# Turning the mixed graph weights K on TensorE in float32 instead of by a DMA transpose

## The reference, cut to what matters

```
x = layernorm(x + first_layer(x, adj))                # h in the kernel, per item [128, 512]
z_l, z_g, v = h @ W_lang.T, h @ W_grav.T, h @ W_V.T
A_l = relu(cos(z_l, z_l)) * not_eye ;  A_g = exp(-|z_g - z_g|^2 / (2 sigma^2)) * not_eye
K_l, K_g = A * adj mask / row sum, for each
K   = w_l * K_l + (1 - w_l) * K_g                     # [128, 128] per item
out = layernorm(h + (K @ v) @ W_O.T)
```

## Time and profile before

| | |
|---|---|
| median of 3 runs | 918.71 us |
| the profiled execution | 919.98 us, its span 918.2 us |
| busy: TensorE, VectorE, ScalarE, GpSimd | 97%, 79%, 63%, 35% |
| granted TensorE clock, mean | 0.994 |
| DMA | 79.55 MB in all; 74 DMA transposes |

### The profile page before, as it was taken

The page is one execution under the profiler, slowest core; times in us unless marked ns, Lnnn a source line. Parts: engine busy times, 40 slices in busy tenths (PEclk is TensorE's granted clock), DMA queues, the critical chain, the costliest instruction groups (busy, mean ns, idle before and its releaser), DMA issues.

```text
span 918.2 us, 18540 instructions
## 1 busy us (share of the span) xinstructions
PE 894.0 (97%) x6706; PEld 535.7 (58%) x6706; DVE 726.8 (79%) x1681; ACT 580.3 (63%) x1069; POOL 321.4 (35%) x306
## 2 busy tenths in 40 slices
PE   8999999999999999999999999999999999999995
PEld 6777886565555555556565656555555555655452
DVE  5888488868788778788788878888878787878867
ACT  6987676697565566665656575757575747472623
POOL 4888353045232333232424242424242424240300
PEclk9999999999999999999999999999999999999998
DMA  8554220201423232323233323233323323241311
GB/s 302 206 183 131 100 93 13 77 5 28 88 70 93 70 91 69 91 71 89 77 92 74 98 68 104 61 101 63 107 57 103 65 95 70 91 65 51 58 46 47
DMA packets 105113, 79.55 MB, mean 87 GB/s; under 512 B 81904, under 2 KB 82032, under 8 KB 103152
## 3 DMA queue, kind: packets, MB, share of 16 engines
q1 hardware_dynamic: 105072, 79.02, 31.5%
HBM read 42.80 MB, written 16.81 MB: 65 GB/s over the span
## 4 chain that ended last, share of the span: by engine, by line
PE 53%; DVE 14%; DMA 6%; ACT 4%; issue 4%; POOL 3%; SPq 1%; DVEq 0%; ACTq 0%; POOLq 0%
PE bank L261 11%; PE bank L263 11%; PE bank L262 11%; PE pair L261 6%; PE pair L263 6%; PE pair L262 6%; DMA arena<-in_x 3%; POOL arena L442 2%; DMA arena<-arena 1%; SPq L333 1%; DVE arena L1783 1%; DMA arena<-rn_dram 1%; DVE stats L1726 1%; DVE arena L1773 1%; DMA rn_dram<-nl 1%
## 5 line engine op out<-in xcount | busy, mean ns | idle before, releaser
L261 PE MATMUL bank<-arena 128*128 128x512 f16 (+2 forms) x1056 | 290.5, 300 | 5.3 <-DMA arena<-arena 4.2
L262 PE MATMUL bank<-arena 128*128 128x512 f16 (+2 forms) x1056 | 291.2, 300 | 0.0
L263 PE MATMUL bank<-arena 128*128 128x512 f16 (+2 forms) x1056 | 291.2, 300 | 0.0
L438 POOL TENSOR_TENSOR arena<-arena 128x512 f32<-128x512 f32 x60 | 76.3, 1271 | 229.5 <-ACT arena L1090 229.5
L261 PE MATMUL pair<-arena 128*128 128x512 f16 (+1 forms) x400 | 150.4, 376 | 0.0
L262 PE MATMUL pair<-arena 128*128 128x512 f16 (+1 forms) x400 | 150.4, 376 | 0.0
L263 PE MATMUL pair<-arena 128*128 128x512 f16 (+1 forms) x400 | 150.3, 376 | 0.0
L261 PEld LDWEIGHTS bank<-arena 128*128 128x128 f16 x1056 | 103.3, 98 | 66.9 <-DMA arena<-arena 5.6
L263 PEld LDWEIGHTS bank<-arena 128*128 128x128 f16 x1056 | 103.3, 98 | 62.9
L262 PEld LDWEIGHTS bank<-arena 128*128 128x128 f16 x1056 | 103.3, 98 | 58.5 <-issue 0.7
L452 POOL TENSOR_TENSOR arena<-arena 128x512 f16<-128x512 f32 x56 | 64.9, 1160 | 170.1 <-ACT arena L1075 170.1
(11 more groups left out here) (368 smaller groups left out, 1880.2 us busy)
## 6 DMA issues: line engine op xcount, KB each, us to landing
arena<-in_x SPq DMA_DIRECT2D x32, 1024.0 KB, 5.6
out_dram<-arena SPq DMA_DIRECT2D x15, 1024.0 KB, 4.3
arena<-rn_dram SPq DMA_DIRECT2D x15, 256.0 KB, 3.8
arena<-arena SPq DMA_TRANSPOSE x74, 3.2
arena<-in_x SPq DMA_DIRECT2D x2, 512.0 KB, 4.6
arena<-in_w_grav_t SPq DMA_DIRECT2D x1, 1024.0 KB, 7.4
arena<-in_w_lang_t SPq DMA_DIRECT2D x1, 1024.0 KB, 5.5
arena<-in_w_v SPq DMA_DIRECT2D x1, 1024.0 KB, 8.4
```

The costliest lines, as they stand in the source:

```text
L261: pe.matmul(dst, ah, bh, start=start, stop=False)
L262: pe.matmul(dst, ah, bl, start=False, stop=False)
L263: return pe.matmul(dst, al, bh, start=False, stop=stop)
L438: pool.tensor_tensor(y[:, b, :], y[:, b, :], xg[slot][:, b, :], ALU.add).then_inc(s["y_ready"], 1)
```

## The change

All groups now turn K the way of group 14: TensorE's `turn_k(g)` stands behind the first quarter of the last value product, VectorE makes both float16 parts out of bank 6. ScalarE's high part of K, VectorE's low part out of SBUF, the tile `k_parts`, the DMA transpose and the semaphore `kT_in` are gone. `project_ahead` writes bank 6 (its item 2), so it waits there for `kT_l_ready`. `k_gravity` (ScalarE) no longer waits for the DMA transpose of the group before.

```diff
@@ SyncE: turn_k removed
-            def turn_k(g):
-                sp.wait_ge(s["kT_l_ready"], g + 1)
-                wait(sp, s["out_ps"], g * GB)
-                sp.dma_start_transpose(kT, k_parts.rearrange("p b n -> p (b n)")).then_inc(s["kT_in"], 16)
             def turn_h(g, slot):
...
-                    if b == HALF and g < NG - 1:
-                        turn_k(g - 1)
@@ TensorE
             def project_ahead(g):
...
                 for b in range(GB):
+                    if b == HALF:
+                        wait(pe, s["kT_l_ready"], g - 1)
                     project_x(g, b, x_h, x_l, bank[4 + b])
...
                 values(g, slot, 2)
+                values(g, slot, 3, range(0, 1))
+                turn_k(g)
+                values(g, slot, 3, range(1, KB))
                 if has_second:
-                    values(g, slot, 3)
                     project_ahead(g + 2)
-                    pe.wait_ge(s["kT_in"], g * 16 + 16)
-                else:
-                    values(g, slot, 3, range(0, 1))
-                    turn_k(g)
-                    values(g, slot, 3, range(1, KB))
-                    pe.wait_ge(s["kT_l_ready"], g + 1)
+                pe.wait_ge(s["kT_l_ready"], g + 1)
                 for b in range(GB):
                     weighted(g, b)
@@ ScalarE
                 act.wait_ge(s["cf_ready"], g + 1)
-                wait(act, s["kT_in"], turned)
...
                     first_norm(g + 1, 1 - slot, 2)
-                    act.wait_ge(s["k_ready"], g + 1)
-                    act.activation(k_parts[:, 0:GB, :], k_mix, ACT.Copy, scale=K_UP).then_inc(s["kT_h_ready"], 1)
                     first_norm(g + 1, 1 - slot, 3)
@@ VectorE
                 v_low(g, 0)
-                if has_second:
-                    dve.wait_ge(s["kT_h_ready"], g + 1)
-                    dve.scalar_tensor_tensor(k_parts[:, GB:, :], k_mix, K_UP, k_parts[:, 0:GB, :], ALU.mult,
-                                             ALU.subtract).then_inc(s["kT_l_ready"], 1)
-                else:
-                    dve.wait_ge(s["kT_ps"], 1)
-                    ...
+                dve.wait_ge(s["kT_ps"], g + 1)
+                dve.tensor_scalar(kT_h, bank[6][:].rearrange("p (b n) -> p b n", b=GB), K_UP, None,
+                                  ALU.mult).then_inc(s["kT_h_ready"], 1)
+                turned_k_low(g)
+                if not has_second:
                     dve.wait_ge(s["hh_ready"], g * GB + GB)
```

More of the change, by code:

```diff
@@ L233, in build @@
             at(next(tile_at), [GB, P]) for _ in range(10))
-        k_parts = at(100 * KIB, [2 * GB, P], F16)
         kT = at(108 * KIB, [2 * GB, P], F16)
@@ L252, in build @@
             dev_ready rn_spread rm_ps sq_ps rn_out rn_in hk_ready e_ready graph_steps cf_steps cf_ready k_ready kg_ready cl_ready
-            v_ps v_h_ready v_l_ready kT_ps kT_h_ready kT_l_ready kT_in o_first out_ps y2_ready
+            v_ps v_h_ready v_l_ready kT_ps kT_h_ready kT_l_ready  o_first out_ps y2_ready
             ln2_var ln2_log ln2_exp ln2_steps o_ready stored stats2_ready nl_steps2 stat1_steps stat2_steps""".split()
@@ L1222, in v_high, with k_gravity @@
                 act.activation(v_h[:, b, :], bank[b][:], ACT.Copy, scale=V_DOWN).then_inc(s["v_h_ready"], 1)
-            def k_gravity(g, turned):
+            def k_gravity(g):
                 act.wait_ge(s["cf_ready"], g + 1)
-                wait(act, s["kT_in"], turned)
                 for b in range(GB):
@@ L1273, in body @@
                 first_roots(g + 1, 0)
-                k_gravity(g, g * 16)
+                k_gravity(g)
                 add_bias(g + 1, 3)
@@ L1318, in last_body @@
                 v_high(g, 1)
-                k_gravity(g, (NG - 2) * 16)
+                k_gravity(g)
                 v_high(g, 2)
-                turned_k_high(1)
+                turned_k_high(g)
                 v_high(g, 3)
@@ L1889, in body @@
                 v_low(g, 0)
-                if has_second:
-                    dve.wait_ge(s["kT_h_ready"], g + 1)
-                    dve.scalar_tensor_tensor(k_parts[:, GB:, :], k_mix, K_UP, k_parts[:, 0:GB, :], ALU.mult,
-                                             ALU.subtract).then_inc(s["kT_l_ready"], 1)
-                else:
-                    dve.wait_ge(s["kT_ps"], 1)
-                    dve.tensor_scalar(kT_h, bank[6][:].rearrange("p (b n) -> p b n", b=GB), K_UP, None,
-                                      ALU.mult).then_inc(s["kT_h_ready"], 1)
-                    turned_k_low(g)
+                dve.wait_ge(s["kT_ps"], g + 1)
[3 more added lines that the diff above has]
+                if not has_second:
                     dve.wait_ge(s["hh_ready"], g * GB + GB)
```

## The result

The changed kernel takes 922.16 us (median of 7 runs, 921.07 to 923.74) against 919.39 us for the kernel before (7 runs, 918.42 to 920.67): ratio 1.003, 95% interval 1.0018 to 1.0042. It is slower by 2.8 us; 921.6 was forecast, 2.9 us above the 918.71 us of three runs from which it started. A second set (experiment 10) gave 922.18 against 919.84, ratio 1.0028 (1.0018 to 1.0038). The profiled execution is one of the quick ones: 921.14 us, span 919.4.

The account below looks back on a forecast made before the run. TensorE's stream, busy 97% of the span, was taken as the bound. 919.98 + 6.16 - 3.48 + 0.25 gave 922.9 us for the profiled execution; for the median, 918.71 + 2.93 = 921.6, range 919.9 to 924.6.

Parts of the forecast that it names:

- Part 1: Four float32 transposes added to TensorE's stream in 14 more groups: 0.44 us each group, 6.16 us, nothing hides it.
- rival d: K's transposes on TensorE run one behind the other at full duration: 15.3 us instead of 6.16, 930.8 us; chance 0.02.
- rival b: Not slower: TensorE's transposes cost only a float16 matmul's 3.1 us, waits give back 3.48, 918.6 us; chance 0.17.
- Part 2: K's parts on VectorE start 0.64 and 1.36 us behind the first transpose; cost nothing, 1.4 us of cover remain.
- Rival (c): A new wait in each group for K's parts or `v_low`: 4 us more, 925.8 us; chance 0.05.
- Part 3: ScalarE's high part and `k_gravity`'s wait removed: ScalarE gets 0.6 us back, worth nothing.
- Part 4: K's DMA transpose removed from SyncE's queue: h's landing gains 1.7 us, TensorE regains 3.48 us of waits.
- The three waits: TensorE's waits for DMA transposes in groups 0 and 2 and at group 14's start cease: 3.48 us regained.
- the fourth: TensorE's wait for a DMA transpose behind group 14, which is unchanged, stays.
- 0.25 us for a k_mix of group 2: Group 2's late k_mix meets the transposes 0.2 us behind their place, costing TensorE 0.25 us.
- Rival (a): Regained waits are the profiled execution's own, from single slow DMAs: 2.2 us or less regained, 922.9 to 925.1; chance 0.16.
- at the upper level throughout: TensorE's granted clock in the kernel before was read as 2.4 GHz over the whole span.

Follow-up runs that it names:

- experiment 10: The changed kernel again, no edit, beside the kernel before: 922.18 us, ratio 1.0028.
- experiment 2: The changed kernel with K's four TensorE transposes issued twice in each of the 16 groups: 929.21 us, ratio 1.0104.
- experiment 3: The changed kernel with one of four transposes left, K's parts made from unturned k_mix, so the output is that of untransposed K: 916.74 us, ratio 0.9965.
- experiments 5: The changed kernel with two spare VectorE products behind K's low part in groups 0 to 13: 921.03 us, ratio 1.0012.
- 6: The changed kernel with four spare VectorE products behind K's low part in groups 0 to 13: 921.43 us, ratio 1.0015.
- experiment 1: The kernel before again, no edit, for a second profile: 919.77 us, ratio 1.0004.
- 4: The kernel before, DMA transpose kept, with K's four TensorE transposes added in groups 0 to 13 and read by nobody: 924.29 us, ratio 1.0053.
- 7: The kernel before with K's DMA transpose issued ahead of h's second one: 922.63 us, ratio 1.0026.
- experiment 8: The kernel before with K's DMA transpose ahead of h's second one and ScalarE's high part of K made earlier: 922.65 us, ratio 1.0022.
- experiment 9: The kernel before with TensorE turning K, without the DMA transpose, in groups 0 and 13 alone: 919.34 us, ratio 0.9996.

## Why the prediction was right

**Part 1, the transposes.** Right to the hundredth: 0.44 us a group by the profile, and experiments 2 and 3 move the time by 7.0 and 5.4 us, where 7.0 and 5.3 were expected. The full duration of 273 ns (rival d) is not what one costs in a stream, and neither is the 0.055 us of a float16 matmul (rival b): the distance of the starts, 0.11 us, is the price. The Trainium skill, "TensorE: Matmul & The Clock Gate", section "Part 4: PE-mode transpose", gives about 275 ns for a transpose in a kernel; the single duration here agrees with it, and the time that experiment 2 adds for each transpose does not.

**Part 2, VectorE.** Right: 0.64 and 1.36 us, no wait in `project_ahead`, idle time of 1.27 us left where 1.4 was forecast. The 0.8 us of waiting for the transposes that was to show on VectorE is 2.05, as the earlier trace rows already had it for group 14; it costs nothing. Experiments 5 and 6 show the cover to be larger than I worked out, 2.5 us and not 1.4: I stopped at the residual's idle time and left out the distance from there to the next group's first product. Rival (c) is out.

**Part 3, ScalarE.** No wait of TensorE in groups 0 to 13 names ScalarE, before or after, as forecast; no run changes this part by itself.

**Part 4, the DMA transpose.** The three waits went, for the 3.48 us that the profiled execution had, and the fourth stayed; h's last transpose goes out 1.9 us earlier against `project_ahead`, where 1.7 was worked out. One term was wrong: 0.25 us for a k_mix of group 2 that would meet the transposes late. It is not late any more; it ends at 317.10, 4.3 us ahead of `project_ahead` at 321.42 as in the other groups (in group 9 alone it is 3.1, which costs nothing):

```profile
315.96 1.14 DVE L1875 SCALAR_TENSOR_TENSOR arena<-arena,cf 128x128 f32<-128x128 f32 x4
```

I had taken its lateness for a slow DMA. The kernel before and experiments 1, 4, 7, 8 and 9 all have a VectorE step of 1.15 to 1.23 us for 0.23 in group 2, and no profile of the changed kernel or of its variants (experiments 2, 3, 5, 6 and 10) has that step: it goes with the program. A slow DMA comes on top in some: the next issue on SyncE's queue follows the small write to `rn_dram` 3.1 us later in the kernel before, where 1.4 is usual, but 1.4 in experiment 9, whose `k_mix` is late all the same. So the wait in group 2, 1.58 of the 3.48 us, came with this lateness, which the change took away along with K's DMA. By the prediction's working either would have ended the wait; no run separates the two, and that the lateness would go was not foreseen. A row of the DMA view of the kernel before, from 305 to 306 us, shows one packet of a queue for instructions moving while the step runs (304.82 to 306.05):

```profile
q14 instruction: 1, 0.01, 1.9%
```

The five other profiles with the step have such a packet inside it too, and those of the changed kernel and its variants have none of that queue from 298 to 312. The two coincide in time; that one causes the other was not tried. Rival (a), by which the waits were the profiled execution's own, falls with experiment 1. One of its prices had a slip: rival (b)'s "some 1.3 us more" of waiting should be 2.93 - 1.84 = 1.1.

**The sum.** The span came out at 919.4 us, not 921.1: 0.79 us ahead of group 0, 0.57 us of small gaps and the 0.25 us just named make 1.6 of these 1.7 us. The clock "at the upper level throughout" was read too roughly: the dip to 0.98 between 100 and 194 us lies in the profile of the kernel before, and the 0.79 us go with it. That the forecast for the median, 921.6, came so near to 922.16 is partly luck. Its difference, 2.93 us, holds two errors of one sign, the gaps left out and the 0.25 that did not come, and the profiles behind the first part say 2.0 and 2.5; the medians say 2.8 and 2.3, and why the first set lies above its profiles is open. The start, 918.71 from three runs, was low: the later sets of the same kernel gave 919.39 to 919.96. The sign and the main terms are not luck: experiments 2, 3 and 4 move each by itself.

## What to carry to other kernels

Where TensorE's stream has no gap, price an added instruction by the distance of the starts in such a stream and count it in full; the shorter path for the data buys back only the waits that the trace shows. Take a second profile before calling a wait an accident: here the same three came back. Before a DMA is moved up a queue, look at what it passes: h's transposes had less than half a microsecond to give, and the move cost more than it brought.

## What had not been expected of the hardware

The same small VectorE step took 1.23 us in group 2 and 0.23 elsewhere, in every profile of the kernel before and its variants, and in none of the changed program. VectorE's low part of K took 1.085 us in place of 0.745 once it began 0.35 us earlier (experiment 8), in all 14 groups. GpSimd's three low parts of h took 3.39 us in group 13 where they took 3.84 before, with VectorE's product out of SBUF beside them gone.
